# Graph layers on one core: TensorE takes gathers and sums by whole chunks, seven runs of each in a group

## What is computed

```python
h = jnp.maximum(_layernorm(x, axis=-1), 0.0)
x = x + _L0_gnn_ref(h, W, a, edge_weight, edge_index)      # attention
h = jnp.maximum(_layernorm(x, axis=-1), 0.0)
...
for i in range(L):                                         # L = 3
    msg = jax.nn.relu(x[src] + edge_attr)                  # 200000 x 128
    aggr = jax.ops.segment_sum(msg, dst, num_segments=N_NODES)
    h = x + aggr
    h = h @ W1[i] + b1[i]
    h = jax.nn.relu(_bn(h, g_mlp[i], be_mlp[i]))
    h = h @ W2[i] + b2[i]
    h = _bn(h, g_out[i], be_out[i])
    if i != L - 1:
        h = jax.nn.relu(h)
    x = h
```

## Time and profile before

| | |
|---|---|
| median of 3 runs | 4149.84 us (4148.54, 4149.84, 4171.91) |
| profiled execution, first to last instruction | 4143.2 us |
| PE / DVE / ACT / POOL busy over the span | 94% / 86% / 74% / 69% |
| layer n = 0, groups 1 to 34 | 1880.0 to 2603.4 us: 33 groups, 21.92 us each |
| layer n = 1 | 2741.6 to 3351.5 us: 33 intervals of 18.34 to 19.39 us, 25 of them 18.34 us, 18.48 us on average |
| layer n = 2 | 3467.8 to 4078.1 us: 18.33 to 19.37 us each |
| granted TensorE clock in those stretches | 0.99, 1.00, 1.00 |

### The profile page before, as it was taken

One profiled execution on the slowest core, in us unless ns is written; L12 is line 12 of the kernel. 1 busy time (PEld: TensorE's weight loads), 2 busy tenths in 40 slices (PEclk: granted clock), 3 DMA queues, 4 the chain that ended last, 5 costly groups with the idle time before them and its releaser, 6 DMA issues.

```text
span 4143.2 us, 151501 instructions
## 1 busy us (share of the span) xinstructions
PE 3880.3 (94%) x50473; PEld 3749.5 (90%) x50475; DVE 3557.9 (86%) x6826; ACT 3079.1 (74%) x7853; POOL 2863.9 (69%) x2594
## 2 busy tenths in 40 slices
PE   3899996899999999979999999899999989999998
PEld 3899996899999999969999999689999968999996
DVE  7799984677777777778888888789999988999997
ACT  4799994677777777767677667678888867888886
POOL 0288883777777777766777777367777736777773
PEclk7888898999999999989999999999999999999999
DMA  9988789898889898868999999689999958999995
GB/s 138 218 274 279 251 280 342 229 249 247 249 248 249 247 252 249 253 208 290 311 322 312 315 311 326 206 268 316 315 319 314 319 189 266 316 314 317 313 323 186
DMA packets 710002, 1132.45 MB, mean 273 GB/s; under 512 B 157402, under 2 KB 535084, under 8 KB 709564
## 3 DMA queue, kind: packets, MB, share of 16 engines
q1 hardware_dynamic: 493068, 787.26, 57.2%
q10 hardware_dynamic: 133200, 176.14, 17.3%
q0 software_dynamic: 83552, 166.66, 12.8%
HBM read 883.83 MB, written 246.33 MB: 273 GB/s over the span
## 4 chain that ended last, share of the span: by engine, by line
PE 66%; POOL 13%; DMA 6%; issue 6%; SPq 5%; DVE 3%; ACT 2%; DVEq 0%; POOLq 0%; ACTq 0%; PEld 0%; PEldq 0%
PE ps L2015 17%; PE ps L1938 14%; PE ps L2035 12%; PE ps L1925 11%; POOL attr_by_slot L874 9%; PE ps L2059 6%; POOL unit_x L938 4%; DMA unit_x<-gin_rows,unit_src 2%; PE ps L2038 2%; PE ps L2106 2%; DMA src_row<-rows_by_group 1%; DMA attr_by_slot<-late_attr,late_ridx 1%; PE ps L2049 1%; DMA abuf<-in_edge_attr 1%; SPq L663 1%
## 5 line engine op out<-in xcount | busy, mean ns | idle before, releaser
L938 POOL DMA_INDIRECT unit_x<-gin_rows,unit_src x1449 | 1457.8, 1006 | 500.2 <-issue 336.3
L874 POOL DMA_INDIRECT attr_by_slot<-abuf,ridx x1020 | 1279.6, 1255 | 486.0 <-issue 310.0
L2015 PE MATMUL ps<-x_parts,src_turned 128*128 128x128 bf16 x15876 | 1138.4, 222 | 26.2 <-ACT ps L1155 22.8
L2015 PEld LDWEIGHTS ps<-x_parts,src_turned 128*128 128x128 fp8e4 x15876 | 949.4, 99 | 71.8 <-issue 29.4
L1155 ACT ACTIVATE ps<-sums 128x512 f32<-128x512 f32 x1512 | 825.8, 546 | 187.2 <-DVE all_split_msg L1677 69.1
L1062 ACT ACTIVATE val<-ps,val 128x128 f32<-128x128 f32 x2597 | 717.9, 375 | 182.7 <-DVE val L1514 182.7
L1670 DVE TENSOR_TENSOR dst_hot<-ps,dl_slot 128x896 fp32r<-128x896 f32 x756 | 816.5, 1080 | 0.2
L1938 PE MATMUL ps<-val,src_hot 128*128 128x129 f32 x5194 | 693.0, 283 | 0.9 <-DVE sums L1454 0.3
L2035 PE MATMUL ps<-all_split_msg,dst_hot 128*128 128x256 f32 x3528 | 649.5, 304 | 10.5 <-DVE all_split_msg L1677 10.5
L1163 ACT ACTIVATE all_split_msg<-ps 128x512 fp32r<-128x512 f32 x1008 | 543.8, 539 | 148.9 <-PE ps L2015 121.1
L1677 DVE SCALAR_TENSOR_TENSOR all_split_msg<-ps,all_split_msg 128x512 fp32r<-128x512 f32 x1008 | 607.7, 615 | 15.8 <-ACT all_split_msg L1163 12.6
(11 more groups left out here) (266 smaller groups left out, 5752.5 us busy)
## 6 DMA issues: line engine op xcount, KB each, us to landing
sums<-attr_by_slot SPq DMA_DIRECT2D x756, 448.0 KB
turned_hot<-rows_by_block ACTq DMA_DIRECT2D x392, 384.0 KB
attr_by_slot<-zeros SPq DMA_DIRECT2D x36, 3136.0 KB
unit_attr<-in_edge_attr SPq DMA_DIRECT2D x204, 448.0 KB
abuf<-in_edge_attr SPq DMA_DIRECT2D x68, 960.0 KB
src_turned<-src_hots SPq DMA_DIRECT2D x504, 112.0 KB
src_row<-rows_by_group SPq DMA_DIRECT2D x252, 112.0 KB
src_hots<-src_turned SPq DMA_DIRECT2D x252, 112.0 KB
```

The lines of the kernel that those rows point to most:

```text
L874: pool.indirect_dma_start(out=attr_table, out_offset=bass.IndirectOffsetOnAxis(ap=ridx[:, g, t0 + t:t0 + t + 1], axis=0), in_=abuf[:, k % ...
L938: pool.indirect_dma_start(out=unit_x[:, half_place(k), t, :], out_offset=None, in_=gin_rows[n], in_offset=bass.IndirectOffsetOnAxis(ap=uni ...
L2015: ins = pe.matmul(ps[:, BANK[h], k * D:(k + 1) * D], src_turned[:, b * P:(b + 1) * P], x_parts[:, part, b, :], start=False, stop=(k == til ...
```

## The change

Only tables of places change. `AHEAD` now gives two gathers ahead of every even half and none ahead of an odd one, and the places of the unit's sum, of the turn of the window and of three additions move with that.

```diff
-AHEAD = ((3, 4), ()) + tuple((h + G_LEAD,) for h in range(2, G_HALVES))
+AHEAD = tuple((h + G_LEAD, h + G_LEAD + 1) if h % 2 == 0 else () for h in range(G_HALVES))
 ...
-SUM_AT = {8: 0, 13: 1}
+SUM_AT = {9: 0, 13: 1}
 BASE_AT = 9
-KEEP_AT = (10, 3)
+KEEP_AT = (12, 3)
 WINDOW_OUT_AT = 2
-WINDOW_TURN_AT = 4
+WINDOW_TURN_AT = 3
 BASES_AT = 1
-WINDOW_AT = 6
+WINDOW_AT = 7
```

## The result

The changed kernel runs in 4164.5 us (median of 20 runs, 4151.4 to 4176.4). The kernel before, on the same chip, runs in 4148.2 us (20 runs, 4137.8 to 4171.9). The ratio is 1.0034, with a 95% interval of 1.0023 to 1.0045. So the change costs 16 us by the medians and 0.34% by the ratio. The forecast was 10 us less than before. The profiled execution spans 4172.7 us against 4143.2 us.

What follows compares the result with a forecast made beforehand. PE was taken to set the 18.34 us cycle in layers 1 and 2, POOL to fill layer 0. A new 18.22 us loop saves 8.4 us, layer 0 2 us: 4149.8 - 10.4 = 4139 us, range 4125 to 4145 us (53%).

Steps and rivals of the forecast that it cites:

- The disturbed ones: Longer groups in layers 1 and 2, bringing the mean cycle from 18.34 to 18.48 us; taken as unchanged.
- POOL's gathers are paced by sums ten halves back: POOL's gathers wait for PE's sums; an even sum coming 0.65 us later was called small against that.
- The loop: Layers 1 and 2: DVE's rests 3 to 8, seed 12, PE's gather 12 to next gather 3, message 3; 18.22 us a group.
- DVE's floor: Layers 1 and 2: DVE without its 0.24 us wait needs 18.10 us a group, however fast PE becomes.
- Pairing on PE: Six newly paired chunks a group save 0.08 us each, so PE's own cycle falls from 18.34 to 17.86 us.
- The moved additions: L1707 moved from half 10 to half 12, some 2.6 us later, so its 0.24 us wait for the unit's sum goes.
- Layer 0: POOL has no time left there; six groups save 0.33 us each, 2 us, the other 30 nothing.
- The slower one: Third rival: gather 12's wait for seed 12 slows the kernel; 4165 to 4170 us for either part, 4185 both; 18%.
- gather 12's wait: PE waits ahead of gather 12 for seed 12, 0.2 to 0.4 us in each group.
- What PE now rides out behind the unit's sum it would meet at once: Layer 0, third rival: DVE's late gathered rows would reach PE, 0.5 us in each of 30 groups, 15 us.
- the bound of 1%: 41 us, about what a measurement can tell from no change; a time within it was given 89%.

Runs made afterwards that it cites:

- six_of_seven: Kernel before and changed kernel, each with GpSimd gathering only six of a unit's seven tiles; one run each, 4131.4 us (before) and 4101.8 us (changed).
- gather12_again: Changed kernel with gather 12 behind sum 8 again; ratio 0.9972 to the kernel before.
- pairs_again: Kernel before with the new AHEAD alone, all other places left as they were; ratio 1.0118 to the kernel before (4 runs).

## Why the prediction was wrong

**The step that failed** is "The disturbed ones, which bring the mean to 18.48 us, I let stand." They didn't stand. I took the spots of before as a fixed toll, and never asked what made them. They were a pause of GpSimd handed on through DVE (L1700) to PE. How much gets through hangs on the length of the pause, on GpSimd's lead, and on the order of PE. In the new order 7.5 us more came through in each of two layers: longer pauses (3.9 to 4.6 us against 2.4 to 2.8 us) at much the same lead, so longer waits of DVE for rows (13.0 against 3.9 us in n = 1), and then PE waits of up to 2.87 us, behind which its clock fell, as it had not behind waits of 1.03 us and less. By the six_of_seven pair, one run each, this is all of the loss but some 1 us. Why the pauses are longer isn't known.

**POOL.** "POOL's gathers are paced by sums ten halves back, and 0.65 us more on an even one is small against that" was wrong in its first half, for n = 1 and n = 2. Opening the gate two halves earlier gave 2 to 3 us a layer, and taking one SBUF operand from L1700 gave 10 and 14 us: POOL was paced by DVE's additions. I had seen POOL full in layer 0, and not added up a group of n = 1, where the earlier trace rows shows 82.22 busy of 110.04 us: with 0.30 us before each of 82 gathers, 106.8 us of it are gone.

**The loop** was right as a mechanism, and its size was off by 0.09 us: 18.22 forecast, 18.31 measured. 0.10 us of it is the hand-off from seed 12 to PE, 0.15 in place of 0.05 us; the rest of the terms came out within 0.02 us. So 70 x 0.12 = 8.4 us became 66 x 0.03 = 2 us. Had only this been off, the time would still have been a little under that of before.

**DVE's floor** was 17.99 and not 18.10 us (gather12_again). What made up the other 0.11 us I haven't read from the traces.

**Pairing on PE** pays about as forecast: 2.06 us for a pair, and an own cycle of PE of 17.90 us, where 17.86 us was forecast. The rule of the Trainium skill, page "TensorE: Matmul & The Clock Gate", section "Back-to-back issue gap", has no such term, and the rows show one: in pairs the change of run is worth 0.08 us a chunk. It is shown through the lengths of runs alone, since PE no longer sets the cycle by itself.

**The moved additions.** L1707's wait went, as forecast, and pairs_again shows what its place was worth: 1.20 us a group, where I had 0.24 + 1.09 = 1.33 us.

**Layer 0** was full of GpSimd's work as forecast, 21.8 us a group before and 21.9 us after. My 2 us can't be told from its spread. **The outer intervals** of each layer cost 2.1 and 2.4 us. I hadn't looked at them, and haven't traced what makes that.

**The rivals.** The slower one gave 4165 to 4170 us for one of its two parts, and 4164.5 us came, but by luck: gather 12's wait is 0.22 us, as forecast, and not what costs. What came was the sentence behind it, on gathered rows ("What PE now rides out behind the unit's sum it would meet at once"), but in n = 1 and 2 and not in layer 0. By the bound of 1% the time is no change, as given at 89%.

**Still open:** what the pause after 112 gathers is, and why it is some 2 to 3.5 us long in two kernels (before, behind the first of a layer, and pairs_again) and mostly some 4 us in the others, the old order with one SBUF operand less among them.

## What to carry to other kernels

When a profile has regular groups and a few longer ones, ask what makes the longer ones before you change the order: they show where a disturbance gets through, and a new order can make them grow. Add up an engine's fixed gaps before you call it idle; one that keeps exact step with another and never waits is held by something that the waits don't show. Taking the two-SBUF-operand addition out of GpSimd's way was worth 0.3 to 0.4% here in either order, in kernels that add a table in place of the gathered rows. Even then the new order is only level with the old (4129.4 and 4129.1 us). The order with gather 12 moved back, whose cycle is 17.99 us, wasn't tried with it.

## What the hardware showed that I had not expected

- In layers n = 1 and n = 2, GpSimd stops for 2.2 to 5.4 us ahead of the 114th indirect DMA of 128 rows and then after every 112, in every kernel here that ran 14 of them in a group. Two more semaphore increments for every seven DMAs didn't move it.
- A gather issued beside a VectorE addition of two SBUF operands goes from 0.94 to as much as 1.86 us (1.79 us in the rows above); beside one with a PSUM operand it stays at 0.94 us. In the changed kernel the addition lasts 1.07 to 1.09 us, also when it begins during a gather.
- In the late groups of the changed kernel, PE waits of 1.99 to 2.87 us were followed by 3 to 4 us with a granted clock of 0.50 to 0.72, a wait of 1.68 us by 1.00.
- In one round the DMAs moved 254 GB/s in the layers and not 318, and all five kernels run in it took some 5100 us. A later round, on a chip of the same number, took 4145.6 us for the kernel before.
